# Adapter with layer norm, 128 sequences: new load order, W1 in 1 KB runs, tables spread by four banks, a store queue that runs three pairs late

## What is computed

```
h   = relu(x[b] @ W1[id] + b1[id])                 # 512 -> 128
y   = x[b] + h @ W2[id] + b2[id]                   # 128 -> 512
out = x[b] + layernorm(y) * gamma[id] + beta[id]   # eps 1e-5
```

## Time and profile before

| what | value |
|---|---|
| time, median of 3 runs | 318.92 us (316.99 to 319.3) |
| the profiled execution's own time | 316.75 us |
| its span, first to last instruction | 315.0 us |
| mean granted TensorE clock | 0.974 of full |
| busy: TensorE, VectorE, ScalarE, GpSimd | 289.5, 289.8, 263.0, 186.2 us |
| moved by DMA | 94.03 MB, mean 298 GB/s |

### The profile page before, as it was taken

How to read it: one execution, slowest core, us unless ns; L and a number is a source line. 1 busy time by engine, 2 the same in 40 slices (tenths; PEclk the granted TensorE clock), 3 DMA queues, 4 the chain that set the end, 5 groups by cost and what they waited for, 6 DMA issues and landing times.

```text
span 315.0 us, 7506 instructions
## 1 busy us (share of the span) xinstructions
PE 289.5 (92%) x2008; PEld 253.8 (81%) x2039; DVE 289.8 (92%) x621; ACT 263.0 (83%) x601; POOL 186.2 (59%) x217
## 2 busy tenths in 40 slices
PE   1757959999999999999999999999999999999972
PEld 1237758889998888998888998888999888999861
DVE  5998856999999999999999999999999999999996
ACT  3977438889988889899989988999989988988872
POOL 2960742666655666565566665656656566665562
PEclk9968779999999999999999999999999999999998
DMA  5999999899999999899898989999898889885324
GB/s 155 332 389 372 293 331 390 276 340 352 358 347 328 321 313 302 302 318 318 292 315 313 299 309 310 318 302 311 290 319 311 315 304 311 286 291 202 116 110 177
DMA packets 56441, 94.03 MB, mean 298 GB/s; under 512 B 3387, under 2 KB 14711, under 8 KB 56273
## 3 DMA queue, kind: packets, MB, share of 16 engines
q1 hardware_dynamic: 56302, 93.41, 87.4%
q10 hardware_dynamic: 99, 0.14, 0.1%
HBM read 44.78 MB, written 33.55 MB: 249 GB/s over the span
## 4 chain that ended last, share of the span: by engine, by line
PE 79%; SPq 10%; issue 3%; DMA 3%; DVE 2%; DVEq 1%; ACT 0%
PE ps_h L504 33%; PE ps_y L525 28%; PE ps_T L488 16%; SPq L287 5%; DMA x_io<-in_x 2%; PE ps_h L497 2%; SPq L269 2%; SPq L257 1%; SPq L282 1%; DVE ps_y L663 1%; DVE ps_y L644 1%; SPq L172 1%; SPq L250 1%; DVEq L172 1%; DMA ids_raw<-in_itok_B 1%
## 5 line engine op out<-in xcount | busy, mean ns | idle before, releaser
L358 POOL TENSOR_TENSOR x_io<-x_io,beta_all 128x512 f32<-128x512 f32 x128 | 163.0, 1284 | 37.3 <-DVE ps_y L644 27.9
L504 PE MATMUL ps_h<-x_T,w_stage 128*128 128x128 f32 x1024 | 126.2, 277 | 0.0
L504 PEld LDWEIGHTS ps_h<-x_T,w_stage 128*128 128x128 f32 x1024 | 121.0, 194 | 0.8
L421 ACT ACTIVATE cut<-ps_y,row_sum 128x512 bf16<-128x512 f32 x128 | 87.9, 687 | 16.3 <-PE ps_y L525 11.4
L676 DVE SCALAR_TENSOR_TENSOR x_io<-ps_y,rstd,x_io 128x512 f32<-128x512 f32 x128 | 90.2, 747 | 2.6 <-DVE rstd L668 0.3
L663 DVE SCALAR_TENSOR_TENSOR ps_y<-ps_y,neg_mean,gamma_all 128x512 f32<-128x512 f32 x128 | 90.3, 750 | 1.7 <-ACT cut L421 1.7
L488 PE MATMUL ps_T<-identity,x_io 128*128 128x128 f32 x512 | 69.4, 280 | 11.2 <-DMA x_io<-in_x 10.1
L488 PEld LDWEIGHTS ps_T<-identity,x_io 128*128 128x128 f32 x512 | 62.2, 145 | 20.8 <-issue 12.6
L401 ACT COPY x_T<-ps_T 128x1024 f32<-128x1024 f32 x64 | 63.5, 992 | 6.7 <-PE ps_T L488 6.5
L525 PE MATMUL ps_y<-w_high,h_high 128*128 x128 | 62.3, 486 | 3.9 <-DVE w_low L625 2.2
L644 DVE SCALAR_TENSOR_TENSOR ps_y<-x_io,b_all 128x512 f32<-128x512 f32 x93 | 62.9, 704 | 0.0
(11 more groups left out here) (67 smaller groups left out, 150.9 us busy)
## 6 DMA issues: line engine op xcount, KB each, us to landing
x_io<-in_x SPq DMA_DIRECT2D x64, 512.0 KB, 5.1
out<-x_io SPq DMA_DIRECT2D x63, 512.0 KB, 3.9
w_stage<-w_all SPq DMA_DIRECT2D x58, 256.0 KB, 3.3
w_stage<-in_L_cond_W SPq DMA_DIRECT2D x12, 256.0 KB, 6.5
x_io<-in_L_cond_W SPq DMA_DIRECT2D x5, 512.0 KB, 7.8
b_all<-in_L_cond_b SPq DMA_DIRECT2D x1, 2560.0 KB, 14.3
w_all<-in_L_cond_W SPq DMA_DIRECT2D x5, 512.0 KB, 7.2
out<-x_io SPq DMA_DIRECT2D x2, 256.0 KB, 2.0
```

What stands on the lines that cost most here:

```text
L358: nc.gpsimd.tensor_tensor(x_slot(t), x_slot(t), of_lang(beta_all, lang), ALU.add).then_inc(x_beta_ready, 1)
L421: nc.scalar.activation(squares[:, t % 2, :], ps_y[t % Y_BANKS][:, :], ACT.Square, scale=-float(H), bias=stat(row_sum, t), accum_out=stat(s ...
L504: last = nc.tensor.matmul(bank[:, b * S:(b + 1) * S], w1_stage[:, 2 * (p % STAGE_PAIRS) + b, c, :], x_T[:, (2 * p + b) % 4, c, :], start=F ...
```

## The change

- SLOTS goes from 20 to 24 (twelve pairs); x_io's W2 staging starts at pair X_FIRST = 7.
- W1 is laid out so that partition p holds the rows 2p and 2p + 1 of each half of W1 side by side: HBM is read in runs of 1 KB. `turn_x` takes columns with step 2 to match.
- Load order: x 0, W2 chunks 0 and 1, x 1, W2 chunk 2, W1 for pair 0, W2 chunks 3 and 4, W1 for pair 1, x 2, and so on; b2_all comes in two halves late, at the start of SyncE's loop. gamma, ids, beta, b1 and b2 rows are loaded by ScalarE's queue.
- gamma and beta are cut in two f32r parts (the rounded one, and a difference with a sign), and spread with a `signed_pick` of 20 rows through four banks (18 copies on ScalarE, two on VectorE). TensorE does the first half of pair 0 between spreads 15 and 16, that of pair 1 behind spread 19.
- The first fourteen tiles (EARLY = 7 pairs) are seeded with x alone (`seed_x`), and b2 is put in by the bf16 product of 30 rows (`without_b2`). `put_b2`, the 128x128 picks and their zeroing go. b2's centring moves from ScalarE to VectorE.
- `copy_w1` runs one pair later, and TensorE's wait for it goes.
- SyncE's loop: x is loaded for pair p + 8, behind the landing of store p - 4, and the store comes last, three pairs late (STORE_LAG = 3).

The core of the diff:

```diff
-SLOTS = 20
+SLOTS = 24
-EARLY = 2
+EARLY = 7
+STORE_LAG = 3
-    w1_rows = w1.rearrange("l (c p) a -> p l c a", c=C)
+    w1_rows = w1.rearrange("l (k p j) a -> p l k (j a)", k=C // 2, j=2)
...
-                    last = nc.tensor.transpose(ps_T[:, t % 2, c, :], x_io[:, t % SLOTS, c * 128:(c + 1) * 128],
-                                               identity[:, :])
+                    last = nc.tensor.transpose(ps_T[:, t % 2, c, :], columns[:, c // 2, c % 2, :], identity[:, :])
...
+            load_x(0)
             load_w2(0)
             load_w2(1)
             load_x(1)
+            load_w2(2)
+            sp.wait_ge(ids_ready, 1)
+            stage_w1(0)
+            load_w2(3)
+            load_w2(4)
             stage_w1(1)
...
+            for n in range(3):
+                load_w1(n)
+            stage_w1(4)
+            load_x(5)
+            for n in range(3, W_CHUNKS):
+                load_w1(n)
+            load_x(6)
+            stage_w1(5)
...
+            load_b2(0)
+            load_x_behind_w2(X_FIRST)
+
+            for p in range(PAIRS - 1 + STORE_LAG):
                 if p + STAGE_AHEAD < PAIRS:
                     stage_w1(p + STAGE_AHEAD)
-                sp.wait_ge(out_ready, 2 * p + 2)
-                sp.dma_start(out_pairs[:, p, :, :], x_pair_slots(p)).then_inc(stored[p % X_PAIRS], 16)
-                if p >= 1 and p - 1 + X_PAIRS < PAIRS:
-                    sp.wait_ge(stored[(p - 1) % X_PAIRS], x_loads(p - 1))
-                    load_x(p - 1 + X_PAIRS)
+                if p == 0:
+                    load_b2(1)
+                ahead = p + X_FIRST + 1
+                if ahead < X_PAIRS:
+                    load_x_behind_w2(ahead)
+                elif ahead < PAIRS:
+                    sp.wait_ge(stored[ahead % X_PAIRS], x_loads(ahead - X_PAIRS))
+                    load_x(ahead)
+                if p >= STORE_LAG:
+                    store(p - STORE_LAG)
...
-                if by_scalar(t):
-                    nc.tensor.matmul(bank, is_lang[:, t:t + 1].broadcast_to([128, S]), parts[:, 2 * H:3 * H],
+                if without_b2(t):
+                    nc.tensor.matmul(bank, is_lang[:, t:t + 1].broadcast_to([3 * L, S]), b2_parts[:, :],
...
+            pe.wait_ge(b2_parts_ready, 1)
+            pe.wait_ge(w2_low_ready, L)
+            for p in range(FIRST, PAIRS):
+                n = p - FIRST
+                for b in range(2):
+                    second_product(2 * n + b, langs[n][b])
+                first_half(p)
```

More of the change, by code:

```diff
@@ L187, in vector_seeds @@
             return t + 1 - scalar_seeds(t)
[L189 to L194, removed]
         def w1_stagings(q):
-            return sum(16 if scalar_copies(r) else 32 for r in range(q % STAGE_PAIRS, q + 1, STAGE_PAIRS))
+            return sum(32 if r < STAGE_HBM else 16 for r in range(q % STAGE_PAIRS, q + 1, STAGE_PAIRS))
         def wait_seed(engine, t):
@@ L449, in step @@
                     copy_x(p + 1)
-                q = p + STAGE_PAIRS - 1
-                if q < PAIRS and scalar_copies(q):
-                    copy_w1(q)
+                if STAGE_HBM <= p + 2 < PAIRS:
+                    copy_w1(p + 2)
                 high_h(p)
@@ L457, in copy_spread, with copy_spreads @@
                 nc.scalar.copy(spread_to(n), spread_bank(n)).then_inc(spread_act, 1)
+            def copy_spreads(first, end):
+                for n in range(first, end):
+                    if n in by_act:
+                        copy_spread(n)
             copy_x(0)
[L460 to L465, removed]
+            copy_spreads(0, L)
+            high_w2(0)
+            copy_spreads(L, HEAD)
             copy_x(1)
+            high_w2(1)
+            copy_spreads(HEAD, 2 * L)
             high_w2(2)
@@ L531, in _, with first_half @@
             turn_x(1)
[L532 to L540, removed]
-                if gone in by_dve:
-                    pe.wait_ge(spread_dve, by_dve.index(gone) + 1)
-                table = parts[:, 0:H] if n < L else parts[:, H:2 * H]
-                nc.tensor.matmul(spread_bank(n), pick[:, n % L, :], table, start=True, stop=True).then_inc(spread, 1)
-            pe.wait_ge(ids_ready, 1)
-            langs = {0: langs_of(pe, 0)}
-            pe.wait_ge(b1_parts_ready, 1)
-            pe.wait_ge(is_lang_ready, 1)
-            pe.wait_ge(spread_act, len(by_act))
-            pe.wait_ge(spread_dve, len(by_dve))
-            for p in range(PAIRS):
-                if p >= FIRST:
-                    n = p - FIRST
-                    if n == 0:
-                        pe.wait_ge(w2_low_ready, L)
-                    for b in range(2):
-                        second_product(2 * n + b, langs[n][b])
+            def first_half(p):
                 pe.wait_ge(x_T_ready, p + 1)
@@ L563, in _ @@
                 first_products(p)
-                if p < PAIRS - 1:
-                    langs[p + 1] = langs_of(pe, p + 1)
-                if p < EARLY:
-                    if p == 0:
-                        pe.wait_ge(b2_parts_ready, 1)
-                    for b in range(2):
-                        put_b2(2 * p + b, langs[p][b])
+            langs = {}
+            pe.wait_ge(pick_ready, 1)
+            pe.wait_ge(gamma_parts_ready, 1)
+            for n in range(2 * L):
+                if n == L:
+                    pe.wait_ge(beta_parts_ready, 1)
+                if n == HEAD:
+                    pe.wait_ge(b1_parts_ready, 1)
+                    pe.wait_ge(is_lang_ready, 1)
+                    first_half(0)
+                gone = n - Y_BANKS
+                if gone in by_act:
+                    pe.wait_ge(spread_act, by_act.index(gone) + 1)
+                if gone in by_dve:
+                    pe.wait_ge(spread_dve, by_dve.index(gone) + 1)
+                nc.tensor.matmul(spread_bank(n), signed_pick[:, n % L:n % L + 1].broadcast_to([2 * L, 128]),
+                                 table_parts[:, n // L, :], start=True, stop=True).then_inc(spread, 1)
+            pe.wait_ge(ids_ready, 1)
+            first_half(1)
+            for p in range(FIRST):
+                langs[p] = langs_of(pe, p)
+            pe.wait_ge(b2_parts_ready, 1)
[5 more added lines that the diff above has]
+                first_half(p)
+                langs[p] = langs_of(pe, p)
             for n in range(PAIRS - FIRST, PAIRS):
```

211 lines of the change are left out of this document (107 added, 104 removed).

## The result

The changed kernel takes 369.94 us (median of 4 runs, 369.37 to 371.95) against 318.61 for the kernel before beside it: ratio 1.163, 95% interval 1.157 to 1.170. Forecast were 327 us in a range of 309 to 342. The profiled execution has a span of 367.5 us.

What follows compares the result with a forecast made beforehand. TensorE bound the kernel before; after the change SyncE's loop would, at 4.8 us a pair against 4.28: from 55.3 to 300.1, TensorE done to 311.9, tail 11.3, span 323.2, 8.2 over 315.0; so 327 us, range 309 to 342.

Steps and rivals of the forecast that it cites:

- the predicted signs: What the trace would show: SyncE waiting over 50 us for stores, later pairs 4.7 to 5.1 us apart, first `second_product` near 27.
- the sign that step 2 costs: TensorE's transposes reading x with step 2: eight taking more than 0.87 us would show a cost; none was forecast.
- P: SyncE's loop: time from a load's issue to the landing of the store behind it, taken as 4.8 us, 52 times.
- Store 0 lands near 55.3 us, 53 to 58: SyncE's loop: landing of the first store, summed from bytes ahead of it; it ends the wait in iteration 4.
- 27 for the first `second_product`: Start of the kernel: ScalarE's 19.0 us of work sets W2 ready at 27 us, 24 to 31, which is 5.2 earlier.
- Priced at nothing: Gamma's and beta's cuts, b2's centring on VectorE, GpSimd's cuts, TensorE's gone wait on `copy_w1` and step-2 transposes: no time.
- the lowest P: SyncE's loop: lower bound of 4.5 us from load issue 0.5, store alone 2.8 and half a megabyte 1.2.
- Rival A: SyncE's loop has room (P up to 4.57), the start's 7.8 us are kept: 311 us, faster; chance 0.25.
- the tail: End of the kernel: time left behind the first products of pair 63, 11.2 us, used as 11.3 in the sum.
- B: The start's gain and the loop's loss cancel (P 4.57 to 4.70): 317 to 321 us; chance 0.10.
- D: Start: W2's low parts still come near 32 us since ScalarE waits for DMA; time as forecast, no separate chance.
- C: TensorE stands half a microsecond per pair and its clock falls, 17 us on top: 344; chance 0.10 shared with P over 5.1.

Runs made afterwards that it cites:

- experiment 1: The changed kernel with the store issued ahead of the wait and the load in SyncE's loop: 350.56 us, ratio 1.104 to the kernel before.
- experiment 2: The kernel before, with SyncE waiting for the previous iteration's store and loading x ahead of the new store, 20 slots, no lag: 369.70 us (1.163).
- experiment 3: The changed kernel with 128-row products, transposes at step 1 and W1 in 512-byte runs, SyncE's loop as changed: 366.32 us (1.154).
- Experiment 12: Changed kernel with store ahead of wait, 128 rows, step 1, 512-byte runs (317.42 us), plus ids loaded first on SyncE's queue: 314.17 us (0.987).
- experiment 4: The kernel before, with only the b1 and b2 products over 30 rows instead of 128: 341.65 us (1.074).
- experiment 6: The kernel before, with only W1 in 1 KB runs and the transposes' columns at step 2: 319.65 us (1.004).
- experiment 9: The changed kernel with STORE_LAG = 2 instead of 3 and nothing else: 360.28 us (1.133).
- experiment 11: The changed kernel with STORE_LAG = 2 and TensorE reading no ids, taking W2 of language 0 for every tile: 349.37 us (1.100).

## Why the prediction was wrong

*Direction and mechanism were right.* The forecast was slower by the wait on the store just issued, and experiments 1, 2 and 3 show that mechanism, once taken away, once put into the kernel before, once alone. Three of the predicted signs were there: a wait on stores over 50 us, DMA share under 0.89 (0.73 from 110 to 290 us), TensorE below 100%. The pairs from 110 to 290 us are 5.10 us apart in the mean, at the edge of the 4.7 to 5.1 forecast. Two signs were not there: pairs ahead of 110 us were 4.54 and 5.05 us apart and not 4.2 to 4.4, and the first `second_product` wasn't near 27 us. And the sign that step 2 costs, over 0.87 us for eight transposes, did come. The 0.35 put on faster and on no change rested on a mean step of at most 4.70 us; of the 51 steps the very shortest was 4.69. *The size was wrong*: +8 forecast, +51 measured.

*The term of the sum that was mis-sized is P*, "I take 4.8, nearest to the load alone and 1.4". It measured 5.46 in the mean. 51 steps of 0.66 more are 33.7 of the 44.3 us between the forecast span of 323.2 and 367.5. The row for it was on the table: 5.3 from the first issue to the second landing in the body. I set it aside because the queue would run empty between turns; it did, and the store still landed 4.9 us after its issue. The argument for less was a sum: a load alone, 3.3, and the spacing of two landings, 1.4. The spacing held (1.32 in the median of the 52 turns). The load did not: with the store issued 0.4 us behind it, it landed after 4.0 us in the median, and so in experiments 2 and 3. Why a load with a store behind it takes 0.7 us longer stays open. The median step is 5.33; five of 6 us and more, up to 7.24, make the rest. Of the 44.3 us between the two spans 1.9 are left, in the end of the chain, which wasn't taken apart.

*The start of the chain was 8.7 us late.* "Store 0 lands near 55.3 us, 53 to 58": the wait of iteration 4 ended at 64.0. I had argued from bytes. In the trace SyncE wasn't short of bytes but held by `stage_w1`, which waits for TensorE's first products, and TensorE's early pairs, each with two 30-row b2 products, were 5.58 us apart (44.43 to 50.01 above). Iteration 3 could issue store 0 only at 59.1 us:

```profile
59.12 0.50 SPq L279 DMA_DIRECT2D out<-x_io  x1
63.51 0.49 SPq L262 DMA_DIRECT2D w_stage<-w_all  x1
64.04 0.59 SPq L247 DMA_DIRECT2D x_io<-in_x  x1
```

With 128 rows, in experiment 3, the early pairs took 4.6 us and the load of iteration 4 came at 60.5.

*The start gave nothing.* "27 for the first `second_product`": 33.61. The sum of ScalarE's work was sound: 19.0 us forecast, and some 18.5 us of it between 6.27 and 32.3 us. What the sum lacks is ScalarE's waits for TensorE, 7.5 us in three pieces (the idle time in brackets):

```profile
10.99 4.99 ACT L479 COPY gamma_all<-ps_y 128x512 f32<-128x512 f32 x10 [3.73 <-PE ps_y L575]
...
20.88 1.01 ACT L424 COPY x_T<-ps_T 128x1024 f32<-128x1024 f32 x1 [1.75 <-PE ps_T L515]
...
25.15 2.05 ACT L479 COPY beta_all<-ps_y 128x512 f32<-128x512 f32 x4 [2.03 <-PE ps_y L575]
```

The first piece hung on the spreads, they on gamma's cut, and that stands behind the ids on VectorE. I priced the ids' load at nothing; issued at 2.13 us behind x 0, two chunks of W2 and gamma's rows, it had landed at 7.7 us of the span instead of at 2.5. Experiment 12 gets 3.3 us back by moving that one line. The other two pieces, 3.8 us for pair 0's transposes and for the spreads behind its first products, no experiment took away; "some waits" was all that the forecast had for them.

*Priced at nothing and not nothing:* the 30-row products, 0.44 us a pair (experiment 4), which I never gave a row or a bound; and step 2, 0.08 us a pair (experiment 6), inside my bounds for eight transposes, 0.87 to 1.7 us. On that place the rule of the Trainium skill (SBUF — State Buffer, on steps of up to four f32) does not hold for these weight loads: 206 ns against 140. The measurement decides. In the changed kernel both lie beside the loop's wait, so they explain some 4 of its 51 us; with the loop free they are 33.

*The estimate from the Trainium skill* of 4.4 us for load and store (DMA: Bandwidth & Descriptors, anatomy of one DMA) was lower still than mine, and further from 5.3. The page fits it to transfers that GpSimd issues, and these are SyncE's. By the rule of the Trainium skill that a completion follows all earlier writes of the engine (same page, "Queues, rings and completion order") a store can't be told done before the load ahead of it. The traces agree: in the 52 turns of the changed kernel the store landed at least 1.2 us after that load, in those of experiment 2 at least 1.0.

*Two slips in the sums.* The lowest P took 1.2 us for half a megabyte; at 386 GB/s, the best rate in the earlier trace rows, it is 1.36, so the lowest P is 4.66 and not 4.5. Rival A, up to 4.57, leaned on that bound and deserved less than 0.25. And the tail is 11.2 us in one place and 11.3 in another.

*Rivals.* A and B needed a step of at most 4.70 in the mean, and are refuted. D, no gain at the start, came true beside the forecast's loop, but not for its reason, a ScalarE that waits for transfers, and its claim that the loop's start hangs on bytes fell with the forecast's. C, the clock, is refuted as well: granted 1.00 from 40 us on in windows of 10 to 50 us up to 350.

## What to carry to other kernels

A buffer that is refilled behind its own store should wait for a store issued at least a whole turn before the wait. Issued at the end of the last turn (the changed kernel, experiment 2) it made each turn a load and a store long, with 20 slots and with 24; issued a turn before, with the new store ahead of the wait (experiment 1), or a turn earlier still (experiment 9), it held nobody. What frees the loop is that distance, not more slots, and a later store shortens it unless the slots grow by as much. Before a small operand is trimmed to the rows it uses, look at what stands on both sides of it in TensorE's stream. And a tiny load at the head of a long chain goes first, ahead of the large ones: one line, 3.3 us here.

## What the runs showed of the hardware that was not expected

- Padding a product with rows of zeros makes it cheaper: over 128 rows a pair takes 4.39 and 4.16 us, over 30 rows 4.97 and 4.46, over 64 rows 4.99 and 4.46 (202.35 to 207.34 to 211.80 us). The loss is some 0.3 us for each short product, 0.2 of it right before and behind it; 23 us in the kernel before.
- Transposes whose weights are read at a step of two f32 load in 206 ns instead of 140.
- Reading two ids from SBUF into an engine's registers takes 0.5 to 2.5 us, and with the load issued ahead of the store it held TensorE some 0.45 us in 17 of 27 b2 pairs (experiments 9 and 11). What sets the length of a read stays open: in experiment 9 reads of TensorE's queue took 0.53 us at a DMA share of 0.05 and at one of 1.18 (in the half microsecond from their start).
